# Layer 3's router and token scatter placed inside its attention, with rows in a ring of four groups, and layer 1's second biases added by VectorE

## What is computed

```python
x = x + tanh(g_xattn[i]) * attention_i(layernorm(x), ctx, ctx)
x = x + tanh(g_ffn[i]) * ffn_i(layernorm(x))
```

```python
h = gelu(einsum('nd,edh->neh', xf, w1) + b1)           # layer 1
y = einsum('neh,ehd->ned', h, w2) + b2
out = (y * norm_g[:, None, None]).sum(axis=1)

router_probs = softmax(x_flat @ router_w.T)            # layer 3
top_k_probs, top_k_idx = top_k(router_probs, 2)
top_k_probs = top_k_probs / (top_k_probs.sum(-1, keepdims=True) + 1e-08)
for e in range(E):
    out_e = new_gelu(x_flat @ w1[e].T + b1[e]) @ w2[e].T + b2[e]
    output = output + cw[:, e:e + 1] * out_e           # cw: the gate of expert e, or 0
```

## Time and profile before

| | |
|---|---|
| median of 3 runs | 3348.3 us (3343.97 to 3349.98) |
| the profiled execution, its own time | 3345.41 us |
| its span, first to last instruction | 3343.6 us |
| busy share of the span | PE 75%, PEld 54%, DVE 47%, ACT 41%, POOL 29% |
| mean granted TensorE clock | 0.88 of 2.4 GHz |

### The profile page before, as it was taken

The page is one execution under the profiler, slowest core; times in us unless marked ns, Lnnn a source line. Parts: engine busy times, 40 slices in busy tenths (PEclk is TensorE's granted clock), DMA queues, the critical chain, the costliest instruction groups (busy, mean ns, idle before and its releaser), DMA issues. The chain is left out here.

```text
span 3343.6 us, 75538 instructions
## 1 busy us (share of the span) xinstructions
PE 2517.0 (75%) x28328; PEld 1799.6 (54%) x28328; DVE 1554.9 (47%) x4219; ACT 1381.0 (41%) x1967; POOL 974.2 (29%) x1036
## 2 busy tenths in 40 slices
PE   5888855539997899899999789982499952249883
PEld 2555533338885555577777545651255531138773
DVE  3555544424443677511121167767567753413332
ACT  2555532213332566544444356650266620024441
POOL 4454436634442121100000000001111126634444
PEclk9999976669997999899999899995599975579997
DMA  3101101136663221000000011110011101146666
GB/s 97 23 22 22 23 21 39 39 110 196 196 193 117 73 61 52 22 0 0 0 0 0 16 39 45 40 40 0 23 29 29 28 26 39 39 128 197 189 192 217
DMA packets 143747, 219.13 MB, mean 66 GB/s; under 512 B 27177, under 2 KB 94513, under 8 KB 143026
## 3 DMA queue, kind: packets, MB, share of 16 engines
q1 hardware_dynamic: 96930, 90.25, 10.6%
q10 hardware_dynamic: 29232, 90.37, 8.6%
q0 software_dynamic: 17408, 36.21, 3.1%
HBM read 157.48 MB, written 43.61 MB: 60 GB/s over the span
## 5 line engine op out<-in xcount | busy, mean ns | idle before, releaser
L1363 DVE TENSOR_REDUCE mx<-psS 128x16 f32<-128x1024 f32 x264 | 322.8, 1223 | 308.1 <-PE psS L986 306.8
L602 POOL DMA_INDIRECT yg<-ysb,yidx x288 | 280.3, 973 | 412.9 <-DVE ysb L1668 180.0
L459 POOL TENSOR_TENSOR ve<-mv,eps 128x4 f32<-128x4 f32 x102 | 20.6, 202 | 1188.1 <-DVE mv L1339 1186.0
L710 ACT ACTIVATE work<-psT 128x1024 f32<-128x1024 f32 x260 | 266.4, 1025 | 196.9 <-PE psT L995 196.1
L704 ACT ACTIVATE work<-work 128x1024 f32<-128x1024 f32 x264 | 278.5, 1055 | 148.7 <-DVE work L1365 145.0
L1365 DVE TENSOR_TENSOR work<-psS,mx 128x1024 f32<-128x1024 f32 x264 | 323.2, 1224 | 9.1
L995 PEld LDWEIGHTS psT<-ident,work 128*128 128x128 f32 x2080 | 234.9, 143 | 153.8 <-issue 90.1
L986 PE MATMUL psS<-kexp,qT 64*64 64x512 f32 x2112 | 292.1, 624 | 31.0 <-DMA kexp<-kT 19.0
L566 POOL DMA_INDIRECT xg<-gio,posi x256 | 252.1, 985 | 187.2 <-DVE gio L1536 108.1
L995 PE MATMUL psT<-ident,work 128*128 128x128 f32 x2080 | 281.8, 279 | 2.3 <-ACT work L710 1.5
L1200 PEld LDWEIGHTS psY<-w_ffn,work 128*128 128x128 f32 x2016 | 247.6, 192 | 9.3 <-DVE work L1645 1.2
(11 more groups left out here) (230 smaller groups left out, 4576.9 us busy)
## 6 DMA issues: line engine op xcount, KB each, us to landing
w_ffn<-in_wmoe ACTq DMA_DIRECT2D x72, 578.0 KB
w_ffn<-in_wmoe ACTq DMA_DIRECT2D x72, 576.0 KB
ctxT<-in_ctxT SPq DMA_DIRECT2D x76, 256.0 KB, 2.7
xin<-xg SPq DMA_DIRECT2D x144, 132.0 KB
kexp<-kT SPq DMA_DIRECT2D x1152, 16.0 KB
gio<-yg SPq DMA_DIRECT2D x16, 512.0 KB, 3.9
work<-yg SPq DMA_DIRECT2D x16, 512.0 KB, 6.4
yg<-ysb,yidx POOLq DMA_INDIRECT x288
```

The lines of the kernel that those rows point to most:

```text
L602: e.indirect_dma_start(out=yg, out_offset=bass.IndirectOffsetOnAxis(ap=yidx[:, b, t:t + 1], axis=0), in_=ysb[:, b, t, :], in_offset=None, ...
L710: e.activation(pT[:, s % 2, :], psT[:, :], ACT.Copy).then_inc(pt_ok, 1)
L1363: e.tensor_reduce(mx[:, :], src, AX, ALU.max).then_inc(s_max, 1)
```

## The change

Dispatch of layer 3 is no longer a stage: on PE, DVE, ACT and POOL a new function `attention_routed(3)` replaces `attention(3)` and `dispatch(3)`, and one barrier goes. It is written out in full, without a loop. In turn `u`, beside the attention of chunk `u`, DVE makes the dispatch's statistics of chunk `u-2`, POOL the reciprocal root and the normalised rows (formerly DVE's), PE the transposition and the logits of chunk `u-3`, ACT two copies out of `psX`. In odd turns from 5 on, group `(u-5)/2` is picked and ranked; in even turns from 6 on it is placed and gated, and POOL issues 8 of its 16 indirect DMAs then and 8 in the turn after. Five turns follow the last chunk for what is still open. Normalised rows lie in `ring`, four buffers of one group. The block table's scratch moves to `work`. In layer 1, the bias matmuls go; DVE adds `ng` times the summed biases, once computed, to x in four instructions per chunk before it waits for the down products.

```diff
         gio = sb("gio", [P, 2, GT, XW])
+        ring = [gio[:, 0, :, :], gio[:, 1, :, :]] + [w_ffn[:, b * GT * XW:(b + 1) * GT * XW].rearrange("p (t d) -> p t d", d=XW)
+                                                     for b in range(1)]
+        gio3 = sb("gio3", [P, GT, XW])
+        ring.append(gio3[:, :, :])
+        lgt = sb("lgt", [P, GT * E])
+        rnk = sb("rnk", [P, GT * E])
...
+            def attention_routed(lay):
+                def norm(c):
+                    b = (c % 2) * LT
+                    e.wait_ge(m["mv"], c + 1)
+                    e.tensor_scalar(mrstd[:, 0, b:b + LT], mmv[:, b:b + LT, 1], EPS, None, ALU.add).then_inc(m["ve"], 1)
+                    e.wait_ge(m["ve"], c + 1)
+                    e.tensor_tensor(mrstd[:, 1, b:b + LT], mrstd[:, 0, b:b + LT],
+                                    mhalf[:, 0:1].broadcast_to([P, LT]), ALU.pow).then_inc(m["rstd"], 1)
+                    if c >= 8 and c % 2 == 0:
+                        e.wait_ge(m[f"sd{c // 2 % 4}"], 16 * 2 * GT * (c // 8))
+                    e.wait_ge(m["rstd"], c + 1)
+                    for t in range(LT):
+                        mm = e.tensor_scalar(ring[c // 2 % 4][:, b + t, 0:D], xs(None, c, t), mmv[:, b + t, 0:1],
+                                             mrstd[:, 1, b + t:b + t + 1], ALU.subtract, ALU.mult)
+                    mm.then_inc(m["xn"], 1)
+
+                def scatter(g, c):
+                    if c == 0:
+                        e.wait_ge(m["seq"], MSTEPS[lay] * (g + 1))
+                    for t in range(GT):
+                        e.indirect_dma_start(
+                            out=xg, out_offset=bass.IndirectOffsetOnAxis(ap=posi[:, g, c, t:t + 1], axis=0),
+                            in_=ring[g % 4][:, t, :], in_offset=None, bounds_check=XROWS - 1)\
+                            .then_inc(m[f"sd{g % 4}"], 16)
+
+                ln(ATT[lay], None, 0)
+                ln(ATT[lay], None, 1)
+                e.wait_ge(gb_ok, lay - lay // 3 + 1)
+                for u in range(CHUNKS + 5):
+                    if u + 2 <= CHUNKS:
+                        ln(ATT[lay], None, u + 2)
+                    if 2 <= u < CHUNKS + 2:
+                        norm(u - 2)
+                    if u < CHUNKS:
+                        x_bias(lay, None, u)
+                    if u >= 6 and u % 2 == 0:
+                        scatter((u - 6) // 2, 0)
+                    if u >= 7 and u % 2 == 1:
+                        scatter((u - 7) // 2, 1)
+                scatter(NG - 1, 1)
...
+                def turned(c):
+                    e.wait_ge(m["xt_ps"], c + 1)
+                    if c >= 1:
+                        e.wait_ge(m["r_ps"], c)
+                    e.activation(v32[:, :], psX[:, :], ACT.Copy).then_inc(m["xt_sb"], 1)
...
+                def rank_out(g):
+                    e.wait_ge(m["rank_ps"], g + 1)
+                    if g >= 1:
+                        e.wait_ge(m["seq"], MSTEPS[lay] * (g - 1) + 21)
+                    e.activation(rnk[:, :], psX[:, GT * E:2 * GT * E], ACT.Copy).then_inc(m["rk"], 1)
...
+                for u in range(CHUNKS + 4):
+                    inside = u < CHUNKS
+                    c = u - 3
+                    for s in range(LT):
+                        if s == 0 and u >= 5 and u % 2 == 1:
+                            expo((u - 5) // 2)
+                        if s == 1 and inside:
+                            q_out(lay, None, u + 1)
+                        if s == 3 and u >= 5 and u % 2 == 1:
+                            rank_out((u - 5) // 2)
+                        if s == 3 and u + 2 <= CHUNKS:
+                            xt(ATT[lay], None, u + 2)
+                        if inside:
+                            p_high(lay, None, *ahead(u, s, 1))
+                            exps(lay, None, *ahead(u, s, 2))
+                        if s == 0 and inside:
+                            v_out(lay, None, u + 1)
+                        if s == 1 and 0 <= c < CHUNKS:
+                            turned(c)
+                        if s == 2 and 0 <= c < CHUNKS:
+                            logits_out(c)
+                        if s == 2 and inside:
+                            k_out(lay, None, u + 2)
+                    if inside:
+                        inverse(lay, None, u)
...
+                e.wait_ge(b2_ps, 1)
+                e.activation(gbo[:, :], psY[:, 0:D], ACT.Copy).then_inc(b2_ok, 1)
...
+                def turn_x(c):
+                    e.wait_ge(m["xn"], c + 1)
+                    e.wait_ge(x_up, K0 + lay * CHUNKS + c + 2 if c + 2 <= CHUNKS else K0 + (lay + 1) * CHUNKS)
+                    for t in range(LT):
+                        mm = e.transpose(psX[:, t * P:(t + 1) * P], ring[c // 2 % 4][:, c % 2 * LT + t, 0:D], ident[:, :])
+                    mm.then_inc(m["xt_ps"], 1)
+
+                def route(c):
+                    e.wait_ge(m["xt_sb"], c + 1)
+                    for t in range(LT):
+                        mm = e.matmul(psX[:, t * E:(t + 1) * E], v32[:, t * P:(t + 1) * P], rw[:, 2, :], start=True, stop=True)
+                    mm.then_inc(m["r_ps"], 1)
...
+                def rank(g):
+                    e.wait_ge(m["seq"], MSTEPS[lay] * g + 18)
...
+                for u in range(CHUNKS + 4):
+                    inside = u < CHUNKS
+                    c = u - 3
+                    for s in range(LT):
+                        if inside:
+                            scores(lay, None, *ahead(u, s, 2))
+                        if s == 1 and inside:
+                            q_proj(lay, None, u + 1)
+                        if s == 1 and 0 <= c < CHUNKS:
+                            turn_x(c)
+                        if s == 2 and 0 <= c < CHUNKS:
+                            route(c)
+                        if s == 3 and 0 <= c < CHUNKS:
+                            e.wait_ge(m["lg"], c + 1)
+                        if s == 3 and u >= 5 and u % 2 == 1:
+                            rank((u - 5) // 2)
+                        if inside:
+                            p_turn(lay, None, *ahead(u, s, 1))
+                        if s == 3 and u >= 5 and u % 2 == 1:
+                            e.wait_ge(m["rk"], (u - 5) // 2 + 1)
+                        if s == 3 and u + 2 <= CHUNKS:
+                            ln_t(ATT[lay], None, u + 2)
+                        if inside:
+                            weigh(lay, None, u, s)
+                        if s == 0 and inside:
+                            v_proj(lay, None, u + 1)
+                        if s == 2 and inside:
+                            k_proj(lay, None, u + 2)
+                        if s == 3 and 0 < u <= CHUNKS:
+                            out_proj(lay, None, u - 1)
+                e.wait_ge(m["seq"], MSTEPS[lay] * (NG - 1) + 20)
+                e.matmul(psO[:, 0:E], ones16[:, :], macc[:, lay // 3, NG % 2, :], start=True, stop=True).then_inc(m["cnt_ps"], 1)
...
                     if hb == 0:
                         e.wait_ge(f["g_done"], val(i, u, 1, K0 - 1))
-                        for t in range(LT):
-                            e.matmul(y[:, t * D:(t + 1) * D], ones[:, :], b2[:, :], start=(t == 0), stop=False,
-                                     skip_group_check=True)
                     e.wait_ge(f["act_ok"], val(i, u, nb, K0 + hb + 1))
                     for t in range(LT):
                         m = e.matmul(y[:, t * D:(t + 1) * D], hbuf[:, n % 4, t * P:(t + 1) * P],
                                      w_ffn[:, 2048 + hb * D:2048 + (hb + 1) * D],
-                                     start=False, stop=(hb == nb - 1), skip_group_check=True)
+                                     start=(hb == 0 and t == 0), stop=(hb == nb - 1), skip_group_check=True)
...
                 e.wait_ge(wffn_in, 32)
+                e.matmul(psY[:, 0:D], ones[:, :], b2[:, :], start=True, stop=True).then_inc(b2_ps, 1)
+                e.wait_ge(b2_ok, 1)
...
+                def stats(c):
+                    b = c % 2 * LT
+                    if c >= 2:
+                        e.wait_ge(m["xn"], c - 1)
+                    for t in range(LT):
+                        e.bn_stats(mst[:, b + t, :], xs(None, c, t))
+                    e.drain()
+                    for t in range(LT):
+                        mm = e.bn_aggr(mmv[:, b + t, :], mst[:, b + t, :])
+                    mm.then_inc(m["mv"], 1)
...
+                for u in range(CHUNKS + 5):
+                    odd = u % 2 == 1 and u >= 5
+                    done = u % 2 == 0 and u >= 6
+                    ga, gb, gn = (u - 5) // 2, (u - 6) // 2, (u - 4) // 2
+                    inside = u < CHUNKS
+                    for s in range(LT):
+                        if inside:
+                            shift(lay, None, *ahead(u, s, 2))
+                        if s == 0:
+                            if 2 <= u < CHUNKS + 2:
+                                x_update(lay, None, u - 2)
```

(29 more changed lines are left out.)

170 lines of the change are left out of this document (144 added, 26 removed).

## The result

The change makes the kernel faster, by far less than forecast: 3306.03 us (median of 4 runs, 3305.17 to 3307.09) against 3348.68 (4 runs beside them), a ratio of 0.9875 with a 95% interval of 0.9858 to 0.9892, so 42.6 us less. The forecast was 144.5 us less, 3201 us. The profiled execution took 3307.09 us (span 3305.3), 106 us more than forecast for it.

The account below looks back on a forecast made before the run. PE was taken to bound layer 3's attention and layer 1's feed-forward, POOL the dispatch; -17.3 (biases), -172.2 (tail) and +45 (turns) sum to -144.5 us, from 3345.4 to 3201 us. Range 3170 to 3238, or 3189 to 3213 if the mechanism holds.

Parts of the forecast that it names:

- what the attention's turn pays: Layer 3's attention: moved dispatch work lengthens its turns, together +45 us; POOL's 8 DMAs per turn counted as 10.2 us.
- Layer 1's biases: Layer 1's feed-forward: removing four fp32 matmuls, 1.08 us of PE in each of 16 chunks, saves 17.3 us.
- The tail: From layer 3's last attention normalise to the last indirect DMA's end: 243.8 us falls to 71.6, -172.2 us.
- The six half groups: Scatter left after the attention: 6 x 8 DMAs of 1.27 us, described as the last of group 5, all of 6 and 7.
- The turn: Attention turns 5 to 15: +3.8 us, 22.2 us on average, odd ones about 1.5 us longer than even.
- Turns 3 and 4: Layer 3's attention: these turns carry only transposition and logits, +2.2 us each.
- Quarter by quarter: Added time per attention turn, scores to scores: quarter 1 +0.5 and +0.1, 2 +1.0 and +0.7, 3 +0.95, 0 +0.55 us.
- quarters 2 and 0: Attention turn: quarter 2 pays logits +1.0 and waiting for ACT's copy +0.7; quarter 0 pays later normalise, +0.55 us.
- PE alone as the bound: Rival, attention: DVE's and ACT's pieces fit gaps, a turn pays only 1.7 us, +21 in all, 3177 us; chance 0.16.
- VectorE held by POOL: Rival, attention: DVE steps wait out POOL's 5.7 us of SBUF work per turn, at most 62 us, 3263 us; chance 0.18.
- The scatter not hidden: Rival: DMAs over 2.1 us beside busy DVE, POOL falls behind, scatter follows attention, 102 us more, 3303 us; chance 0.04.
- The clock: Rival, attention: PE's clock drops from 2.4 to 1.2 GHz, 15.4 us per turn, 246 for 16, 3447 us; chance 0.04.

Follow-up runs that it names:

- The best version: Changed kernel with indirect DMAs in pairs per quarter and GpSimd's bias, layernorm and normalised rows put between the pairs: 3244.03 us, ratio 0.9697 to the kernel before.

## Why the prediction was wrong

**The step that failed** is in what the attention's turn pays. I counted the 8 DMAs as 10.2 us of POOL, found room for them on POOL's queue, wrote that SP's queue is not touched, and let them cost PE nothing. They cost ten turns 100.1 us, the difference of 314.2 and 414.3: the run with the scatter behind everything shows it, and the extra scatters in the kernel before show 9.1 per turn with nothing else of the change there. It isn't a mis-sized term; the term was missing. What the runs showed in its place is that PE does not start its matmuls, or the others do not learn of their end, while a long row of indirect DMAs is issued beside SP's. I asked of each moved instruction what its queue pays and what waits for its result, not what other engines do while it runs.

**The profile of before held the hint.** In layer 0's dispatch GpSimd scatters beside PE's shared feed-forward. From that timeline:

```profile
581.76 1.51 PE L1124 MATMUL psY<-w_ffn,work 128*128 128x128 f32 x8 [4.50 <-DVE x_sb L1573]
...
586.39 0.97 POOL L566 DMA_INDIRECT xg<-gio,posi  x1 [0.30 <-issue]
...
588.30 0.75 DVE L1573 SCALAR_TENSOR_TENSOR x_sb<-psY,tg,x_sb 128x512 f32<-128x512 f32 x1 [6.69 <-remote]
```

The product was ready at 583.3, VectorE began at 588.30, a microsecond behind the last DMA; the view of waits has six of these, 31.4 us, and 29.2 us of "issue" ahead of the weights of L1124. I read layer 3's dispatch alone for the price, where PE is idle and nobody would notice.

**Point by point.**
- Layer 1's biases: -17.3 forecast, -15.1 measured. PE was saved the matmuls; in the profile after, the down products (L1438) into `psO` wait 3.9 us for ScalarE (8 times).
- The tail: 71.6 forecast, 75.1 measured. Twice, four normalised rows took 3.1 us where I took 1.9, inside the bounds. The six half groups are those of groups 5, 6 and 7 whole, 48 DMAs in the trace; the sum has the right number and its words name one too few.
- The turn: 22.2 on average forecast, 21.4 without scatter, odd ones 1.6 longer than even (forecast 1.5). Turns 3 and 4 took 20.57, forecast 20.7. Quarter by quarter the mechanism was right: in the run without scatter PE waits 1.48 us for the ranks' mask (forecast 1.3) and 0.50 for the copy ahead of the logits. It was 0.8 us per turn too dear, most of it in quarters 2 and 0 with 0.3 each: from first to last normalise 314.2 instead of 323.1.
- PE alone as the bound, turns of 20.2: even turns, 20.7, come near it, odd ones wait for the ranks. (With the tail at its lower bound, 4 us less, this rival gives 3173 and not the 3170 of the range; nothing hangs on it.)
- VectorE held by POOL: the lock exists and held it for some 1.1 us per turn, not 5.7, with scatter and without. Turns without scatter came out shorter than forecast all the same.
- The scatter not hidden: its total, 3303, is what came out, and its mechanism did not. The DMAs did not slow down, POOL did not fall behind; they were hidden under the attention, which they made longer by as much as they took.
- The clock: 0.95 before and 0.87 after in the windows of the attention. It fell to half, but only behind each stall, 0.82 over the ten turns; that is a consequence of the stalls, which begin at 1.00, and takes a share of their price. Over whole turns it did not fall to half.
- 8.4 us at the first normalise: 2.2 are the biases' smaller gain. The rest is of the size by which executions differ: in kernels that are alike up to that point it lay between 2414.8 and 2422.2.

So of the 169 us by which the tail became shorter, the scatter alone takes 100 back in the turns. The best version, 3244.03, gets some 60 of them back by order alone: its attention is 354.3 us long, first normalise to last.

## What to carry to other kernels

An engine that looks idle is not free room: before moving work under a busy stage, find a stretch of the same profile in which both already run together, and read there what every other engine waits for, the waits for "issue" and "remote" first. Where indirect DMAs must run beside a dense PE stage with other DMAs, keep the rows short, with GpSimd's own work between them (two pairs per turn cost 0.1 us here, a row of four 2.9), and count the rows in the trace, since waits that are already met merge them. Measure an added instruction in the kernel before, with nothing else changed: one such run gave here in one number what the whole profile after only hinted at.
